# Mix stage: the output products' remainders on two halves of the rows, a ScalarE copy for them, and two tops placed ahead of the variance

## The reference

```
y = ys[:, 0] + ys[:, 2, :, ::-1] + (the two column directions)
y = _ln_cf(y, out_norm_w, out_norm_b)
y = y * jax.nn.silu(z)
out = jnp.einsum('cd,bdhw->bchw', out_proj_w, y)
return x + out
```

## Time and profile before

| | us |
|---|---|
| three runs | 9250.34, 9255.11, 9254.0 |
| median | 9254.0 |
| profiled execution | 9256.15 |
| its span, first to last instruction | 9254.4 |

### The profile page before, as it was taken

One profiled execution on the slowest core, in us unless ns is written; L12 is line 12 of the kernel. 1 busy time (PEld: TensorE's weight loads), 2 busy tenths in 40 slices (PEclk: granted clock), 3 DMA queues, 4 the chain that ended last, 5 costly groups with the idle time before them and its releaser, 6 DMA issues. The chain is left out here.

```text
span 9254.4 us, 103902 instructions
## 1 busy us (share of the span) xinstructions
PE 8642.6 (93%) x26448; PEld 4648.4 (50%) x26448; DVE 7377.0 (80%) x8229; ACT 6091.9 (66%) x7440; POOL 3295.4 (36%) x1853
## 2 busy tenths in 40 slices
PE   7899998999989998899988999889998899988999
PEld 3336743367433674336733367333673336733476
DVE  6987779877798777987679876798767987689876
ACT  6765677656776567765677556775567755677566
POOL 2870028600286002860038600385003850038400
PEclk9999999999999999999999999999999999999999
DMA  1320013200132001320013200232002320023200
GB/s 53 111 87 13 10 56 112 80 13 10 57 111 82 11 11 59 115 76 10 11 63 111 76 10 11 65 116 71 8 12 68 111 73 8 11 72 114 66 8 12
DMA packets 286693, 503.21 MB, mean 54 GB/s; under 512 B 142155, under 2 KB 143215, under 8 KB 253431
## 3 DMA queue, kind: packets, MB, share of 16 engines
q1 hardware_dynamic: 286199, 497.81, 17.9%
HBM read 467.99 MB, written 29.47 MB: 54 GB/s over the span
## 5 line engine op out<-in xcount | busy, mean ns | idle before, releaser
L1400 DVE TENSOR_TENSOR pl<-pf,ph 128x1024 fp32r<-128x1024 f32 x1024 | 1254.3, 1225 | 1007.1 <-ACT ph L1020 999.5
L1253 DVE TENSOR_TENSOR_SCAN h<-ps,h,dbu 128x512 f32<-128x512 f32 x1536 | 1884.2, 1267 | 59.8 <-POOL dbu L1087 29.9
L1087 POOL TENSOR_TENSOR dbu<-bs,du 128x1024 f32<-128x1024 f32 x768 | 1808.1, 2369 | 54.1 <-POOL du L1078 54.1
L1020 ACT ACTIVATE ph<-pf 128x1024 fp32r<-128x1024 f32 x1024 | 1085.3, 1060 | 750.3 <-PE ps L708 750.0
L885 ACT ACTIVATE ps<-dt,negA 128x512 f32<-128x512 f32 x1536 | 1037.5, 687 | 684.8 <-DVE h L1253 684.8
L1014 ACT ACTIVATE pf<-ps 128x1024 f32<-128x1024 f32 x1024 | 1050.4, 1026 | 530.7 <-PE ps L695 513.3
L1066 POOL MEMSET pad<- 128x66 f32 (+1 forms) x64 | 7.2, 200 | 3853.2 <-DVE fa L1429 3853.0
L1384 DVE TENSOR_REDUCE mx<-ps 128x1 f32<-128x512 f32 x1792 | 1168.6, 683 | 78.8 <-PE ps L606 62.5
L1261 DVE TENSOR_TENSOR hc<-h,ps 128x1024 f32<-128x1024 f32 x768 | 937.9, 1221 | 110.3 <-PE ps L487 19.7
L487 PE MATMUL ps<-xhl,selr 128*128 128x512 f32 x1536 | 768.1, 585 | 238.8 <-DVE hc L1261 238.6
L1072 POOL TENSOR_TENSOR dt<-dt,ze 128x1024 f32<-128x1024 f32 x256 | 604.0, 2359 | 1061.3 <-ACT dt L878 1061.3
(11 more groups left out here) (204 smaller groups left out, 14540.6 us busy)
## 6 DMA issues: line engine op xcount, KB each, us to landing
bs<-rows SPq DMA_DIRECT2D x256, 1024.0 KB, 5.1
bs<-rows SPq DMA_DIRECT2D x512, 256.0 KB, 6.1
xa<-in_x SPq DMA_DIRECT2D x130, 256.0 KB, 2.9
xb<-in_x SPq DMA_DIRECT2D x130, 128.0 KB, 3.0
out<-fa SPq DMA_DIRECT2D x64, 256.0 KB, 2.1
rdb<-rden SPq DMA_DIRECT2D x56, 192.0 KB, 3.4
out<-fa SPq DMA_DIRECT2D x64, 128.0 KB, 2.4
xhl<-ct SPq DMA_DIRECT2D x256, 8.0 KB
```

The costliest lines, as they stand in the source:

```text
L1020: A(ph[:, mp % 2, :, :], pf[:, mp % 2, :, :], ACT.Copy).then_inc(S["ph_ready"], 1)
L1087: pool.tensor_tensor(dbu[:, q, :, :], bs[par][:, q, :, :], du[:, r:r + 1, :].to_broadcast([P, 2, T]), ALU.mult).then_inc(S["dbu_ready"], 1)
L1253: dve.tensor_tensor_scan(h[:, j, ::step], ps[:, 2 + e, ::step], dbu[:, q, e, ::step], h[:, j, end:end + 1], ALU.mult, ALU.add)\
L1400: TT(pl[:, mp % 2, :, :], pf[:, mp % 2, :, :], ph[:, mp % 2, :, :].bitcast(F32), ALU.subtract)\
```

## The change

1. LOADS gets two more entries, which put `wo1`'s 64 rows a second time into rows 64-127.
2. In the output products, the two on `oa` come first (banks 2 and 3), then the two on `ob`: bank 2 with rows 0-63 of `wo1` and `ob`, bank 3 with rows 64-127 of both. So each of the two now has 64 rows.
3. Rows 64-127 of `ob` are a copy of rows 0-63, made by ScalarE at the end of its step (for step -1 too), behind its wait for `phl_ready` of the step and new waits for `gated_ready` and (from step 0) `mixed`. It signals the new semaphore `twice_ready`. TensorE waits for it ahead of all four output products, VectorE from step 0 on ahead of `deviate`.
4. The first two tops move from behind the variance to ahead of it on TensorE.
5. `ob` is no longer zeroed by GpSimd; the counts of `rows_zero` follow.

```diff
+                 (wo1[R:P, R:C], w_out[P:C, 0:P]), (wo1[R:P, 0:R], w_out[P:C, P:C]),
...
@@ TensorE, step @@
+                    early = "p" in which and not (isinstance(c, int) and c == 0)
                     if "p" in which:
                         pe.wait_ge(S["gated_ready"], i * 2 + 4)
-                        for bank, lo, hi in ((2, R, C), (3, 0, P)):
+                        pe.wait_ge(S["twice_ready"], i + 1)
+                        halves = ((2, R, C, slice(0, R)), (3, 0, P, slice(R, P)))
+                        for bank, lo, hi, _ in halves:
                             mm(ps[:, bank, :], wo0[:, lo:hi], oa[:, :], start=True, stop=False)
-                            m = mm(ps[:, bank, :], wo1[:, lo:hi], ob[:, :], start=False, stop=True)
+                        for bank, lo, hi, at in halves:
+                            m = mm(ps[:, bank, :], wo1[at, lo:hi], ob[at, :], start=False, stop=True)
                         m.then_inc(S["mixed"], 1)
+                    if early:
+                        early_top(c, 0)
+                        early_top(c, 1)
                     if "n" in which:
                         pe.wait_ge(S["sq_ready"], n * 2 + 2)
                         mean_of(1, sqa[:, :], sqb[:, :], "var_ready")
-                    early = "p" in which and not (isinstance(c, int) and c == 0)
-                    if early:
-                        early_top(c, 0)
-                        early_top(c, 1)
@@ ScalarE, step @@
                         act.wait_ge(S["phl_ready"], i + 2)
                         if isinstance(c, int) and c == 0:
                             split_theta(i, 0)
+                    if "n" in which:
+                        act.wait_ge(S["gated_ready"], j * 2 + 4)
+                        if not (isinstance(c, int) and c < 0):
+                            act.wait_ge(S["mixed"], j)
+                        A(ob[R:P, :], ob[0:R, :], ACT.Copy).then_inc(S["twice_ready"], 1)
@@ GpSimd @@
-                zero_rows(b * 4 + 6, b + 2, (yt[R:P, :, :], sqb[R:P, :], nb_[R:P, :], ob[R:P, :]))
+                zero_rows(b * 3 + 5, b + 2, (yt[R:P, :, :], sqb[R:P, :], nb_[R:P, :]))
@@ VectorE, step @@
                         dve.wait_ge(S["gated_ready"], j * 2 + 2)
+                        if not (isinstance(c, int) and c < 0):
+                            dve.wait_ge(S["twice_ready"], j)
                         deviate(n, pad0[:, bass.ds((c + 1) * T, T)], yt[0:R, 1 - par, :])
```

More of the change, by code:

```diff
@@ L205, in build @@
             "hc_ready", "summed", "y0_added", "y1_added", "zero_h",
-            "yt_ready", "mix_link", "gated_ready", "mixed", "x1_ready", "phi_ready", "phf_ready", "phh_ready", "phl_ready",
+            "yt_ready", "mix_link", "gated_ready", "twice_ready", "mixed", "x1_ready", "phi_ready", "phf_ready", "phh_ready", "phl_ready",
             "gt_ready", "gth_ready", "gtl_ready",
@@ L626, in step @@
                         if isinstance(c, int) and c < 0:
-                            pe.wait_ge(S["rows_zero"], b * 4 + 6)
+                            pe.wait_ge(S["rows_zero"], b * 3 + 5)
                             pe.wait_ge(S["row_one"], b + 2)
                         mm(ps[:, 0, :], avg[:, :], yt[:, q, :], start=False, stop=True).then_inc(S["mean_ready"], 1)
+                    early = "p" in which and not (isinstance(c, int) and c == 0)
                     if "p" in which:
                         pe.wait_ge(S["gated_ready"], i * 2 + 4)
-                        for bank, lo, hi in ((2, R, C), (3, 0, P)):
+                        pe.wait_ge(S["twice_ready"], i + 1)
+                        halves = ((2, R, C, slice(0, R)), (3, 0, P, slice(R, P)))
+                        for bank, lo, hi, _ in halves:
                             mm(ps[:, bank, :], wo0[:, lo:hi], oa[:, :], start=True, stop=False)
-                            m = mm(ps[:, bank, :], wo1[:, lo:hi], ob[:, :], start=False, stop=True)
+                        for bank, lo, hi, at in halves:
+                            m = mm(ps[:, bank, :], wo1[at, lo:hi], ob[at, :], start=False, stop=True)
                         m.then_inc(S["mixed"], 1)
+                    if early:
+                        early_top(c, 0)
+                        early_top(c, 1)
                     if "n" in which:
```

## The result

The changed kernel took 9274.99 us (median of 8 runs, 9252.54 to 9294.44) against 9252.33 (8 runs, 9249.62 to 9255.11): ratio 1.003, 95% interval 1.002 to 1.004. On another chip it was 9282.59 against 9256.54, 1.0026 (1.0016 to 1.0037). So it is slower by 0.25 to 0.3%, some 23 to 26 us; 36 were forecast. The eight runs of the kernel before lie within 6 us (its 21 to 30 runs on each of four other chips within 19 to 23), those of the changed kernel in three heaps near 9253, 9273 and 9294 (on the other chip from 9259.5 to 9295.5, without such heaps). Two of the 27 runs of the kernel before that stand beside the first four experiments took 15750 and 18365 us and are left out of the comparison. The profile was taken of the fastest one: 9252.54 us, span 9250.1, shorter than that of the kernel before although the median is longer. Read naively it says "no change".

What follows compares the result with a forecast made beforehand. Two rings closed at once bound the mix: TensorE's stream (about 11.3 us) and the da-to-da ring. Losses of 4.43 us an image, 35.4 over 8 images, plus 1.1 for loads, gave 9290 us, range 9264 to 9318.

Steps and rivals of the forecast that it cites:

- rival 3, changes paid: Output products: the remainder pair costs one product, 0.86 us saved, 0.40 paid for row changes; 9272; chance 0.12 for both forms.
- the copy behind phl in step 7: Step 6 into 7: output products wait for phl 0.60, 0.28 and copy 0.61 after ob; +1.49 us an image.
- the copy ahead of step 0's products: Step -1 into 0: output products wait for copy 0.61 and a second hand-over, starting 0.66 us later.
- step 1 late through `split_theta`: Step 0 into 1: ScalarE copies only after gth, thf, thc; products +0.85 us, tops ahead of the variance +0.47.
- three slots, not four: Four remainder passes on TensorE overlap by one pass: 0.43 us saved, 0.40 lost to row changes, net 0.03 per step.
- the chain through the copy: Steps 1 to 6, variance to variance through rstd, phl, copy, output products and tops: 11.62 us, setting the step.
- the da ring: Steps 1 to 6, from one da subtraction to the next: 11.40 us after the change, 11.81 at a loop's end.
- the interval between variances below 11.4: Sign in the profile after that would show the forecast wrong; steps 1 to 6 were forecast about 0.25 us longer.
- The 0.28 ahead of the copy: ScalarE's delay from phl's end to the copy's start, with three waits: 0.28 us.
- rival 4: 0.28 us ahead of the copy too long; 0.2 less in four intervals and step 7: 9283; chance 0.60 together with forecast.
- Rival 1: The output products' halves do not overlap; TensorE loses 0.40 us per step: 9315; chance 0.17.
- rival 2: TensorE's stream sets the step, copy falls in ScalarE's idle time; 0.43 us back in each of 64 steps: 9227; chance 0.04.

Runs made afterwards that it cites:

- the first four experiments: Kernel before with early tops alone, copy alone, 64-row halves alone; and changed kernel with three unread products ahead of step 0's output products, 16 us above kernel before.
- the filler in step 0: Changed kernel plus three unread products on TensorE ahead of step 0's output products; median 16 us above the kernel before of the same chip.

## Why the prediction was right, and where it was not

The time is in the range and the direction is right. The sum behind it is not: two errors of opposite sign stand in it, and that they left 23 to 26 us of 36 is partly luck. This is the sum by its own terms, against an image of each kernel at full clock (103.84 and 102.05 us):

```
us an image                          forecast   measured   rival 3, changes paid
first subtraction to variance of 0     +0.63      +0.22        +0.20
variance of 0 to that of 1             +1.29      +1.00        +0.86
variance of 1 to that of 6             +1.05      -0.29         0
variance of 6 to nmx                   +1.46      +0.86        +1.03
sum                                     4.43       1.79         2.09
```

- Right: the direction, and that TensorE alone does not set steps 1 to 6. Steps 2 to 5 changed by 0.04 us or less while each lost 0.48 of TensorE's work and gained a copy.
- Right in place: the copy behind phl in step 7 (+1.49 forecast; 1.54 against 0.08, so +1.46), the copy ahead of step 0's products (+0.66; the products stood 0.05 us behind ob's end before, 648.25 to 648.30, and stand 0.80 behind it now, 647.96 + 0.74 = 648.70 to 649.50: +0.75), step 1 late through `split_theta` (+0.85 and the tops; step 1 grew by 0.62 once the halves are in).
- The term that was mis-sized: "the first pass of the second can run beside the second pass of the first, not earlier: three slots, not four", net 0.03 us per step. Measured, the pair costs one product: 1.06 us with one change of rows against 1.92 on the same rows. Net 0.48 (3.54 to 2.95, less 0.1 of open load), next to the 0.46 of the third rival's second form, whose 9272 is the nearest of all the forms to 9275. (Its 2.15 us an image is 2.09 by its own terms.) The price of the changes of rows was right: 3.83 - 3.54 and 0.1 of open load, 0.39, against 0.40. The Trainium skill, TensorE: Matmul & The Clock Gate, section The mechanism, has products on different row groups start 4 ns apart. The trace agrees: the pair is in flight within 0.70 us, of which one pass takes 0.69. It is the rule that I should have set against my order of issue.
- It follows that the chain through the copy (11.62 forecast) was below the da ring. The five intervals between variances, forecast at 58.29, summed to 56.96 (11.25, 11.77, 11.36, 11.38, 11.21), against 57.24 before. "or the interval between variances below 11.4" was a sign of being wrong, and it came true. It was badly set, though, since three of the five were below 11.4 before (11.31, 11.37, 11.39). The 0.28 ahead of the copy is 0.18 (683.99 to 684.17), as rival 4 had it. The extra wait on VectorE is 0.07 (0.65 for 0.58), 0.09 forecast. The loads cost 1.3 us (TensorE's first product at 35.73 instead of 34.47), 1.1 forecast.
- From the first subtraction to nmx 4 to 5 us more were forecast; at equal clock it is 1.8. With the overlap put right the sum would be 2.09.
- Missing altogether: the clock. The chain and the loads make 15.6 us (8 x 1.79 + 1.3). What is above that in the two medians, 7 to 10 us, is what the filler in step 0 gave back. A low image costs the changed kernel 3.4 to 4.8 us (1.5 where only step -1 fell) and the kernel before up to 1.9, but the kernel before has more of them. In the two profiles of the changed kernel the clock's part of the mix was 5 us less and 4 us more than in that of before. So the share of the clock in the difference of the medians rests on the run with the filler, not on these sums.
- Rival 1 (no overlap) fell by the first profile, rival 2 (faster) by steps 2 to 5, which gave nothing back.

What stays open: why the rest of the span varies by 23 us from profile to profile, and so how much of the difference between two medians is the change's own. The mix is settled to a few tenths of a microsecond at a given clock; which images are low in which run is not.

## What to carry to other kernels

Two products of 64 rows of contraction on separate halves of the rows cost one here, but a change of the number of rows cost 0.2 us each way, so group them. On a ring that another engine closes the pairing gives nothing. A copy that feeds them must be issued where its input is ready, not at the end of the engine's stream behind a wait that it doesn't need, and every wait for it must stand at the instruction that needs it. A longer idle stretch of TensorE ahead of products can also mean that they run at half clock in some executions. Compare steps at the same clock before believing one profile, above all when it is the fastest run, and check that the row taken as "full clock" is so to its end.

## What the runs showed of the hardware

- Two 64-row products of 128x512 f32 (four passes) on rows 0-63 and 64-127: 1.06 us; on the same rows 1.92; two 128-row ones, also four passes, 1.71 to 1.89.
- The output products mostly at 1.2 instead of 2.4 GHz: 3.3 us for four passes instead of 1.89, after a gap of 2.25 us. With the gap filled (three products nobody reads) step 0 did not run low in any of 8 images; with both gaps filled, 8 of 8 heads ran at full clock, in the kernel before too.
- The same program's profiles differed by 30 us (9250.1 and 9280.2) with steps 1 to 5 equal to 0.02 us; the mean granted clock was 0.986 and 0.983.
